# Two PSUM banks for the weighted sums, two instead of three for the second-pass scores, in an attention and mixture-of-experts layer

## The reference

```
kqv  = xn @ W_kqv.T                    # k, q, v: 16 heads of 16 columns
s    = q k^T / 16 + slope_h * (n - s)  # alibi bias
attn = softmax(s) v                    # 8 sequences x 16 heads x 1024 x 1024 scores
moe  = top-2 of 8 experts of width 352 (scale 2.5) + a shared expert of width 704
out  = x + attn + moe(xn)
```

## Time and profile before

| | |
|---|---|
| median of 3 runs | 2472.49 us (2471.0 to 2473.5) |
| the profiled execution | 2481.54 us, its span 2479.7 us |
| front and experts | from 0 to about 1130 us of the span |
| attend | from about 1130 us to the end |
| busy over the span | PE 97%, DVE 77%, ACT 63%, POOL 31% |

### The profile page before, as it was taken

One profiled execution on the slowest core, in us unless ns is written; L12 is line 12 of the kernel. 1 busy time (PEld: TensorE's weight loads), 2 busy tenths in 40 slices (PEclk: granted clock), 3 DMA queues, 4 the chain that ended last, 5 costly groups with the idle time before them and its releaser, 6 DMA issues.

```text
span 2479.7 us, 53641 instructions
## 1 busy us (share of the span) xinstructions
PE 2413.8 (97%) x19426; PEld 1494.1 (60%) x19426; DVE 1902.0 (77%) x2889; ACT 1554.7 (63%) x3212; POOL 780.8 (31%) x901
## 2 busy tenths in 40 slices
PE   8999999997999999988999999999999999999998
PEld 7888888887999999963333333333333333333333
DVE  6666666656546555468999999999999999999994
ACT  3333333334333333325888888888888888888888
POOL 2222233224232222220113333333333333333333
PEclk9999999998999999986999999999999999999999
DMA  6999877661332222233434344443434343434321
GB/s 188 181 168 179 173 125 149 138 116 43 87 85 76 74 74 76 69 73 60 76 56 93 71 79 79 77 81 74 84 75 81 72 87 67 90 65 92 64 57 42
DMA packets 177924, 229.05 MB, mean 92 GB/s; under 512 B 42828, under 2 KB 127436, under 8 KB 177656
## 3 DMA queue, kind: packets, MB, share of 16 engines
q1 hardware_dynamic: 153048, 172.02, 35.9%
q0 software_dynamic: 22448, 50.56, 8.4%
q10 hardware_dynamic: 2176, 3.02, 0.3%
HBM read 131.47 MB, written 93.66 MB: 91 GB/s over the span
## 4 chain that ended last, share of the span: by engine, by line
PE 54%; DVE 1%; ACT 0%; issue 0%; DVEq 0%
PE p_o L1423 24%; PE p L1413 19%; PE p L1400 9%; PE p L1433 2%; DVE part L1255 1%; PE p L1406 1%; ACT probs L1375 0%; ACT o_sb L1363 0%; DVE neg L1263 0%; DVE att L1282 0%; DVE att L1302 0%; DVE rec L1279 0%; DVEq L1248 0%
## 5 line engine op out<-in xcount | busy, mean ns | idle before, releaser
L1255 DVE TENSOR_REDUCE part<-p 128x2 f32<-128x1024 f32 x1024 | 1240.2, 1221 | 82.2 <-PE p L1400 54.9
L1375 ACT ACTIVATE probs<-p 128x512 f32<-128x512 f32 x2048 | 1109.9, 598 | 170.6 <-PE p L1413 128.6
L1400 PE MATMUL p<-k_op,q_op 50*128 50x512 f32 x2048 | 762.2, 463 | 14.0 <-DVE part L1255 10.9
L1413 PE MATMUL p<-q_op,k_op 51*128 51x512 f32 x2048 | 761.4, 453 | 0.8 <-DVE part L1255 0.4
L1423 PE MATMUL p_o<-probs,v_op 128*32 128x256 f32 x8192 | 657.6, 393 | 4.4 <-ACT o_sb L1363 1.0
L1413 PEld LDWEIGHTS p<-q_op,k_op 51*128 51x128 f32 x2048 | 313.7, 186 | 421.6 <-ACT probs L1375 358.4
L1423 PEld LDWEIGHTS p_o<-probs,v_op 128*32 128x32 f32 x8192 | 163.5, 108 | 358.3 <-ACT probs L1375 280.4
L1400 PEld LDWEIGHTS p<-k_op,q_op 50*128 50x128 f32 x2048 | 307.0, 189 | 29.3 <-DVE part L1255 26.2
L1206 POOL TENSOR_TENSOR att<-o_t,rec 128x256 f32<-128x256 f32 x63 | 39.0, 619 | 814.4 <-DVE rec L1271 814.4
L828 POOL DMA_INDIRECT xe<-xn_scratch,ids x135 | 144.7, 1072 | 364.4 <-DMA ids<-lists_scratch 341.0
L921 ACT ACTIVATE gated_e<-p_gate 128x352 f32<-128x352 f32 x135 | 62.6, 464 | 191.7 <-PE p_gate L859 136.9
(11 more groups left out here) (186 smaller groups left out, 4044.1 us busy)
## 6 DMA issues: line engine op xcount, KB each, us to landing
k_op<-qk_scratch SPq DMA_DIRECT2D x192, 128.0 KB
q_op<-qk_scratch SPq DMA_DIRECT2D x192, 128.0 KB
yr_scratch<-y SPq DMA_DIRECT2D x135, 128.0 KB
qk_scratch<-k_op SPq DMA_DIRECT2D x32, 512.0 KB
qk_scratch<-q_op SPq DMA_DIRECT2D x32, 512.0 KB
v_scratch<-v_op SPq DMA_DIRECT2D x16, 1024.0 KB
v_op<-v_scratch SPq DMA_DIRECT2D x32, 512.0 KB, 9.3
x<-in_x SPq DMA_DIRECT2D x16, 512.0 KB, 4.8
```

Of the source, the lines that this page charges most:

```text
L1255: v.tensor_reduce(part[c_ % 2][:, kh, :, qb], p1[use % 2][:], AX.X, ALU.max, negate=True).then_inc(s["s1_read"], 1)
L1375: a.activation(probs[kb % 4][:, h], p2[use % 3][:], ACT.Exp).then_inc(s["s2_read"], 1)
L1400: return t.matmul(p1[use % 2][:, x], q_op[u][lo:lo + S1_ROWS, pair, q0:q0 + P], k_op[u][lo:lo + S1_ROWS, pair, kh * 512:(kh + 1) * 512], s ...
L1413: t.matmul(p2[use % 3][:], k_op[u][lo:lo + S2_ROWS, pair, kb * P:(kb + 1) * P], q_op[u][lo:lo + S2_ROWS, pair, half * HQ:(half + 1) * HQ], ...
```

## The change

The eight banks are dealt out anew: two for `p_o`, one for each half of a group, and two instead of three for the ring `p2`. All counts that belong to the ring's depth go down by one (the first credit, the release values of `read`, of `send_max` and of `turned_copy`), and bank numbers are taken mod 2. The first products of a half no longer wait for the copy of the half before but for the one before that, which had read the same bank. No instruction is added, removed or moved in any engine's list, nor any transfer.

```diff
--- before.py
+++ after.py
@@ -1076,8 +1076,8 @@
         fin = sb("fin", [P, 3, NK, D])
         slot_i = sb("yslot_i", [P, 2, NBLK], I32)
         p1 = [ps(f"p1_{i}", [P, 2, 512]) for i in range(2)]
-        p2 = [ps(f"p2_{i}", [P, 512]) for i in range(3)]
-        p_o = ps("p_o", [P, HQ])
+        p2 = [ps(f"p2_{i}", [P, 512]) for i in range(2)]
+        p_o = [ps(f"p_o{i}", [P, HQ]) for i in range(2)]
 
         names = ("passed ones_in init s1_ps s1_read neg_ok s2_ps s2_read pv_done o_ok rec_ok "
                  "pool_c o_st0 o_st1 att_ok o_out base_in0 base_in1 yg_in0 yg_in1 fin_base fin_y "
@@ -1137,7 +1137,7 @@
                     load_operand(sp, keep, scratch, k_op[u], q_op[u], v_op[u], g, u, i)
 
             def send_max(g, u, half, use):
-                sp.wait_ge(s["s2_read"], use + 4)
+                sp.wait_ge(s["s2_read"], use + 3)
                 for pair in range(PAIRS):
                     for x in range(2):
                         r = 64 * x + S2_ROWS - 1
@@ -1274,7 +1274,7 @@
 
                 b, hg = g // (H // GH), g % (H // GH)
                 dve.wait_ge(s["s2_ps"], use + 1)
-                ot = p2[use % 3][:].rearrange("p (q h c) -> p q h c", q=4, h=GH)
+                ot = p2[use % 2][:].rearrange("p (q h c) -> p q h c", q=4, h=GH)
                 r = rec[(2 * g + half) % 2]
                 v.reciprocal(r[:], ot[:, :, :, HD]).then_inc(s["rec_ok"], 1)
                 dve.wait_ge(s["rec_ok"], 2 * g + half + 1)
@@ -1336,7 +1336,7 @@
         @block.scalar
         def _(act):
             a = nc.scalar
-            act.sem_inc(s["s2_read"], 3)
+            act.sem_inc(s["s2_read"], 2)
             act.sem_inc(s["o_ok"], 1)
             act.sem_inc(s["pv_done"], NK)
 
@@ -1345,7 +1345,7 @@
                 act.wait_ge(s["s2_ps"], use + 1)
                 if g:
                     act.wait_ge(m_in[half], g * (32 * PAIRS))
-                a.copy(m_row[half][:], p2[use % 3][0:8 * PAIRS, 0:P]).then_inc(s["s2_read"], 1)
+                a.copy(m_row[half][:], p2[use % 2][0:8 * PAIRS, 0:P]).then_inc(s["s2_read"], 1)
 
             def turned_copy(g, half, use):
 
@@ -1353,14 +1353,14 @@
                 act.wait_ge(s["s2_ps"], use + 1)
                 if x_no >= 2:
                     act.wait_ge(s["att_ok"], x_no - 1)
-                ot = p2[use % 3][:].rearrange("p (q h c) -> p q h c", q=4, h=GH)
+                ot = p2[use % 2][:].rearrange("p (q h c) -> p q h c", q=4, h=GH)
                 a.copy(o_t[x_no % 2][:], ot[:, :, :, 0:HD + 1]).then_inc(s["s2_read"], 1)
-                act.wait_ge(s["s2_read"], use + 4)
+                act.wait_ge(s["s2_read"], use + 3)
                 act.sem_inc(s["o_out"], 1)
 
             def output_copy(g, half):
                 act.wait_ge(s["pv_done"], (g * 2 + half) * NK + 2 * NK)
-                a.copy(o_sb[half][:], p_o[:]).then_inc(s["o_ok"], 1)
+                a.copy(o_sb[half][:], p_o[half][:]).then_inc(s["o_ok"], 1)
 
             row_copy(0, 0, 0)
 
@@ -1372,7 +1372,7 @@
                     if h == 0:
 
                         act.wait_ge(s["pv_done"], g * (2 * NK) + (half * NK + kb - 3 + NK))
-                    a.activation(probs[kb % 4][:, h], p2[use % 3][:], ACT.Exp).then_inc(s["s2_read"], 1)
+                    a.activation(probs[kb % 4][:, h], p2[use % 2][:], ACT.Exp).then_inc(s["s2_read"], 1)
                     if n == OWN_TURN:
                         row_copy(g, use + 1, 1)
                     elif n == TURN_AT and has_next:
@@ -1403,24 +1403,24 @@
             def turn_max(g, half, use):
                 pe.wait_ge(s["neg_ok"], g * CHUNKS + PAIRS * (half + 1))
                 pe.wait_ge(s["s2_read"], use + 1)
-                t.transpose(p2[use % 3][0:8 * PAIRS, 0:P], neg[half][:].bitcast(F32), ident[:]).then_inc(s["s2_ps"], 1)
+                t.transpose(p2[use % 2][0:8 * PAIRS, 0:P], neg[half][:].bitcast(F32), ident[:]).then_inc(s["s2_ps"], 1)
 
             def score(u, use, n):
 
                 half, kb, h = n // HALF, n % HALF // GH, n % GH
                 pair, x = divmod(h, 2)
                 lo = 64 * x
-                t.matmul(p2[use % 3][:], k_op[u][lo:lo + S2_ROWS, pair, kb * P:(kb + 1) * P],
+                t.matmul(p2[use % 2][:], k_op[u][lo:lo + S2_ROWS, pair, kb * P:(kb + 1) * P],
                          q_op[u][lo:lo + S2_ROWS, pair, half * HQ:(half + 1) * HQ],
                          start=True, stop=True).then_inc(s["s2_ps"], 1)
 
             def products(g, u, half, kb, side):
 
                 if kb == 0 and side == 0:
-                    pe.wait_ge(s["o_ok"], g * 2 + (half + 1))
+                    pe.wait_ge(s["o_ok"], max(1, g * 2 + half))
                 cols = slice(side * SIDE, (side + 1) * SIDE)
                 for h in range(GH):
-                    ins = t.matmul(p_o[32 * h:32 * h + 32, cols], v_op[u][:, kb, VW * h:VW * h + VW],
+                    ins = t.matmul(p_o[half][32 * h:32 * h + 32, cols], v_op[u][:, kb, VW * h:VW * h + VW],
                                    probs[kb % 4][:, h, cols], start=(kb == 0 and side == 0), stop=(kb == NK - 1),
                                    skip_group_check=True)
                 if side:
@@ -1430,7 +1430,7 @@
                 pe.wait_ge(s["o_ok"], g * 2 + (half + 2))
                 pe.wait_ge(s["s2_read"], use + 1)
                 for q in range(4):
-                    ins = t.transpose(p2[use % 3][:, q * P:(q + 1) * P], o_sb[half][:, q * P:(q + 1) * P], ident[:])
+                    ins = t.transpose(p2[use % 2][:, q * P:(q + 1) * P], o_sb[half][:, q * P:(q + 1) * P], ident[:])
                 ins.then_inc(s["s2_ps"], 1)
 
             pe.wait_ge(keep["ones0_in"], 32)
@@ -1444,7 +1444,7 @@
 
             def group(g, u, turn, has_prev, has_next):
                 nu, nt = following(u, turn)
-                read = lambda n: use2(g, n) + 4
+                read = lambda n: use2(g, n) + 3
                 for n in range(UNITS):
                     half, l = divmod(n, HALF)
                     if n == 0 and not has_prev:
@@ -1472,7 +1472,7 @@
 
                         side = l % GH // 2
                         k_ago = n // GH - 1
-                        pe.wait_ge(s["s2_read"], use2(g, 0) + 3 if k_ago < 0 else read(GH * k_ago + GH - 1))
+                        pe.wait_ge(s["s2_read"], use2(g, 0) + 2 if k_ago < 0 else read(GH * k_ago + GH - 1))
                         if k_ago < 0:
                             products(g - 1, (u + 2) % 3, 1, NK - 1, side)
                         else:
```

## The result

The changed kernel takes **2617.8 us** (median of 4 runs, 2615.7 to 2622.4) against 2472.4 before: ratio 1.0572, 95% interval 1.0549 to 1.0596, so 5.7% slower (the two medians alone give 1.0588). The forecast was 2606 us, range 2560 to 2645. The two profiled spans differ by 2617.0 - 2479.7 = 137.3 us, where the sum of the prediction gave 134. The medians differ by 145; the profiled execution of before lay 9 us above its own median, that of after 1 us.

What follows compares the result with a forecast made beforehand. TensorE's list was taken to set the pace, 1.24 us a pair. Each half gains 1.68 + 0.28 + 0.11 = 2.07 us: +128 over 31 groups, -1 start, +7 last group, +134 on 2472.5, so 2606 us, range 2560 to 2645.

Steps and rivals of the forecast that it cites:

- Ordinary pairs: Pairs of scores: odd weight load waits for the previous pair's second exponential; 1.345 us per pair, +0.105, +1.68 a half.
- All four terms (0.54, 1.09, 0.05, 1.01): Two-pair time: start of exponentials, both exponentials, hand-over to the weight load, late load to next pair; 2.69 us.
- Turn of the maxima: `turn_max` must wait for the exponential of unit 4 instead of 3; three pairs take 4.74 us, extra +0.28 a half.
- the prediction's list of signs: Expected profile after: odd loads 0.3 to 0.45 late, `turn_max` 2.6 after units 2/3, copies 22.9 us apart, clock 1.00.
- Turn of the output: Score 15 waits for the bank `turned_copy` empties, loading 0.55 late; two pairs take 2.80 against 2.47, extra +0.11 a half.
- A half: Half of a group: ordinary pairs 1.68, turn of maxima 0.28, turn of output 0.11, together +2.07 us on 20.84.
- Last group: Only scores and products; two pairs took 2.23 us, now the same 1.345 tie: +7.3, turns +0.5, `p_o` -0.6, so +7.
- The span: Whole profiled execution: 31 groups of two halves +128, start -1, last group +7, together +134 us, 2481.5 to 2615.5.
- the offset between profile and median: Median of the runs before lay 9 us below the profiled execution; predicted median 2472.5 + 134 = 2606 us.
- Part 1, the second `p_o` bank: First products of a half no longer wait for `output_copy`, already covered by `turn_max`; -0.6 us in the last group only.
- the rival of the falling clock: New TensorE gaps drop the granted clock from 2.4 to 1.2 GHz: 29 us per group so spent, 900 if lasting; chance 0.05.
- The argument from the last group: Against a falling clock: last group has less TensorE work per time, pairs of 1.12 us, yet its clock is 1.00.

Runs made afterwards that it cites:

- Experiments 5 and 6: Changed kernel with each second-pass exponential cut from 512 to 448 (5) or 384 (6) columns, for timing only: 2572.0 us, ratio 1.0372, and 2529.8 us, ratio 1.0190.
- experiment 9: Kernel before with first pass cut to 128 of every 512 keys in one `p1` tile, plus two `p_o` banks and three for `p2`: 2612.0 us.
- experiments 8: Control: kernel before with first pass cut to 128 of every 512 keys in one `p1` tile, two banks left free: 2538.1 us.
- the moved turn: `turn_max` moved behind the products of its unit: 2585.0 us, ratio 1.0456, in the changed kernel; 2481.4 us, ratio 1.0031, in the kernel before.
- experiment 10: Kernel before with first pass cut to 128 of every 512 keys in one `p1` tile, one `p_o` bank and four for `p2`: 2517.9 us.

## Why the prediction was right

- **Ordinary pairs**: forecast 2.69 us for two, measured 2.67. All four terms (0.54, 1.09, 0.05, 1.01) were in the trace of before, the last two from the one place where the same wait already occurred. Experiments 5 and 6 moved one term and the pairs followed.
- **Turn of the maxima**: 4.74 forecast, 4.79 measured, by errors that partly cancel. The exponential of unit 4 starts 2.04 after units 2/3 (1901.25 - 1899.21), not 1.97, since the copy ahead of it comes at 1.56 (1900.77), not 1.50. The hand-over from that exponential to the transpose's weights is 0.12 (1901.85 to 1901.97), not 0.05, and the transpose starts 0.03 behind them. So `turn_max` stands at 2.79, where the prediction's list of signs has 2.6. The products follow 0.20 later, not 0.31, and take most of that back.
- **Turn of the output**: 2.80 and 2.79.
- **A half**: 2.07 forecast, 2.16 measured. Of the 0.09 between them 0.05 is the turn. The rest is that late and punctual pairs are not half and half, as the average of 1.345 has it: of the 11 ordinary pairs in the half from 1899.21 on, 6 are late and 5 punctual, since each turn restarts the alternation, and 6 x 1.44 + 5 x 1.24 is 14.84, against 11 x 1.345 = 14.80.
- **Last group**: +7 forecast; its two halves went from 19.24 and 18.23 us to 22.96 and 20.71, +6.2.
- **The span**: 61 halves x 2.17 = 132.4, last group 6.2, start -1.3: the 137.3 seen. The median lies 12 us above the forecast, of which 3 are the sum. The rest is the offset between profile and median, 9 us in the kernel before, which I took over and which is 1 us in the kernel after; each comes from a single profiled execution, so it may be mere scatter, and no term of the mechanism explains it.
- **Part 1, the second `p_o` bank: the value was right (nothing), the reason was not.** The products behind `turn_max` did wait 0.11 us for the copy; experiment 9 showed, with the shortened first pass, that taking the wait away gives nothing, since a score two steps later waits for the same ScalarE.
- **The clock** stayed at 1.00 in the full groups (granted clock of 1200 to 2560 us), so the rival of the falling clock did not occur. The Trainium skill (TensorE: Matmul & The Clock Gate, "A second HAM failure mode: psum-queue depth-cycling"), which the prediction cites for it, has the clock swing between its levels in a kernel that cycles through PSUM banks; the trace of this kernel, which does so too, shows no swing. The argument from the last group was weaker than I took it for, all the same: the kernels of experiments 8 and 9 stayed at the lower level for long with less work in each pair. But none of the profiled executions fell back to it in the full groups once it had risen.

Not tried: the second `p_o` bank beside a ring of three with the full first pass, since PSUM has no ninth bank for it; and the moved turn with a ring of two and a single `p_o`.

## What to carry to other kernels

A ring's depth is paid for by overlap: before taking a buffer away, write down when its reader is done and when the next-but-one writer wants it, both from the start of a period; here the load is ready at 1.63 + 0.05 and was wanted at 1.24 + 0.24, so two pairs lose 0.20 us, where 2.67 - 2.48 = 0.19 was measured. Look in the trace for a spot where the tighter wait already occurs (here behind the turn, which used a slot of the ring), for it gives the hand-over and the restart cost in place. And a wait that one takes away is worth something only if what stands behind it isn't held by the same late engine.

## What the runs showed of the hardware

TensorE's granted clock can stay at its lower level for long although the profile shows TensorE busy without a break. In experiment 9, whose `max_half` streams 128 columns instead of 512, the stretches read (columns as in the earlier trace rows):

```profile
1200.00:1300.00 100.00, 100.00 (x611) 36.87 (x605) 21.89 (x58) 56.79 (x108) 7.67 (x9) 0.50 0.27 44
...
1400.00:1500.00 100.00, 100.00 (x609) 36.96 (x608) 21.88 (x58) 56.84 (x108) 25.64 (x32) 0.50 0.26 48
1500.00:1600.00 100.00, 94.98 (x941) 39.28 (x944) 34.66 (x91) 86.56 (x167) 39.54 (x50) 1.00 0.40 73
```

The level was 0.50 (1.2 GHz) to about 1500 us, TensorE being busy 100% in the stretches shown, and then 1.00 to the end of the full groups, with TensorE busy 95%. In the kernels before and after the same low level ended between 1150 and 1160 us. Single executions of experiment 9 differ by 133 us (2499 to 2632), and so do those of experiment 10, whose mean granted clocks differ with them. The busy share doesn't show this; the granted clock does, and so do the number of products in 100 us (609 against 941) and the length of a score's row (0.79 us at 1302.85, against 0.50). What made the level rise late in these kernels no run shows.

A second point: the hand-over from ScalarE to TensorE was not one number here. A score's weights follow the exponential by 0.05 us (1813.51 to 1813.56); the weights of `products` behind `output_copy`, and those of `turn_max` behind an exponential, follow by 0.12 (1812.51 to 1812.63, 1901.85 to 1901.97).
